# Mixer: backward turns beside the state sums, inputs a state ahead, one Silu block per pair, convolutions in the tail

## The reference, cut to what matters

```python
EMB, DS, DC, EXP = 128, 16, 4, 2          # DI = 256 channels, 16 states
def _mamba(x, in_w, conv_w, conv_b, xproj_w, dt_w, dt_b, A_log, D, out_w):
    xc, z = jnp.split(jnp.einsum('ble,ie->bli', x, in_w), 2, axis=-1)
    xc = _silu(causal_conv(xc, conv_w) + conv_b)          # DC = 4 taps
    dt, Bm, Cm = jnp.split(xc @ xproj_w.T, [DTR, DTR + DS], axis=-1)
    dt = jax.nn.softplus(dt @ dt_w.T + dt_b)
    A = -jnp.exp(A_log)
    dA = jnp.exp(dt[..., None] * A)                       # one decay per state
    dBx = dt[..., None] * Bm[:, :, None, :] * xc[..., None]
    h = dA_t * h + dBx_t                                  # the scan over time
    y = sum over the 16 states of h * C  + xc * D
    return (y * _silu(z)) @ out_w.T
out_f = _mamba(out, ...f weights)
out_b = _mamba(out[:, ::-1], ...b weights)[:, ::-1]
```

## Time and profile before

| what | us |
|---|---|
| median of 3 runs (3865.65 to 3873.80) | 3869.11 |
| the profiled execution, its time | 3876.9 |
| its span | 3875.1 |
| first scan of the mixer starts at | 1649.25 |
| last pair of the mixer ends at | 3383.34 |

### The profile page before, as it was taken

How to read it: one execution, slowest core, us unless ns; L and a number is a source line. 1 busy time by engine, 2 the same in 40 slices (tenths; PEclk the granted TensorE clock), 3 DMA queues, 4 the chain that set the end, 5 groups by cost and what they waited for, 6 DMA issues and landing times. The chain is left out here.

```text
span 3875.1 us, 60191 instructions
## 1 busy us (share of the span) xinstructions
PE 2899.2 (75%) x18634; PEld 2085.9 (54%) x18635; DVE 2717.1 (70%) x4018; ACT 2280.7 (59%) x4020; POOL 2070.9 (53%) x1444
## 2 busy tenths in 40 slices
PE   3999999521999960578888878888888887769934
PEld 2555555321666640256556656666566665669933
DVE  3788887442444447288888898888889898967643
ACT  1566665420333320499888888898888888522232
POOL 1011111265222222389889898888889898612234
PEclk6999999655999985799999999999999999879955
DMA  3444444411111136012222222222222222120050
GB/s 94 88 87 87 87 91 83 118 55 43 39 39 39 39 94 125 26 62 71 75 72 73 72 75 67 71 70 68 75 72 72 70 75 66 54 83 24 15 152 14
DMA packets 219679, 269.61 MB, mean 70 GB/s; under 512 B 36684, under 2 KB 139110, under 8 KB 214554
## 3 DMA queue, kind: packets, MB, share of 16 engines
q1 hardware_dynamic: 199106, 247.08, 24.6%
q0 software_dynamic: 12256, 18.82, 1.4%
q10 hardware_dynamic: 8064, 0.55, 0.2%
HBM read 219.79 MB, written 54.22 MB: 71 GB/s over the span
## 5 line engine op out<-in xcount | busy, mean ns | idle before, releaser
L1736 POOL TENSOR_TENSOR resid_x<-s_ux,s_B_rows 128x1024 f32<-128x1024 f32 x256 | 604.8, 2363 | 154.5 <-PE s_y L2084 154.4
L2013 DVE TENSOR_TENSOR_SCAN resid_x<-s_back_decay,s_back_in 128x1024 f32<-128x1024 f32 x256 | 584.2, 2282 | 143.9 <-PE s_back_in L2071 143.8
L2005 DVE TENSOR_TENSOR_SCAN resid_x<-s_dA,resid_x 128x1024 f32<-128x1024 f32 x256 | 582.4, 2275 | 114.3 <-ACT s_dA L1828 106.2
L2084 PE MATMUL s_y<-identity,resid_x 128*128 128x128 f32 x4096 | 560.9, 282 | 5.9 <-POOL resid_x L1744 5.9
L2084 PEld LDWEIGHTS s_y<-identity,resid_x 128*128 128x128 f32 x4096 | 499.7, 146 | 84.1 <-issue 52.1
L1744 POOL TENSOR_TENSOR resid_x<-resid_x,s_C_rows 128x1024 f32<-128x1024 f32 x192 | 453.3, 2361 | 44.4 <-DVE resid_x L2005 44.2
L1828 ACT ACTIVATE s_dA<-s_dt,s_A 128x510 f32<-128x510 f32 x512 | 330.4, 677 | 132.4 <-DVE resid_x L2005 132.1
L2020 DVE TENSOR_TENSOR resid_x<-resid_x,s_C 128x1024 f32<-128x1024 f32 x320 | 383.5, 1198 | 23.9 <-PE s_C L2061 23.3
L467 DVE TENSOR_REDUCE a_row_max<-a_maxscores 128x2 f32<-128x512 f32 x512 | 335.9, 683 | 79.5 <-PE a_maxscores L545 79.2
L1849 ACT ACTIVATE resid_x<-s_uT,s_bT 128x256 f32<-128x256 f32 x864 | 370.3, 496 | 10.3 <-issue 9.3
L391 ACT ACTIVATE a_probs<-a_scores 128x1024 f32<-128x1024 f32 x256 | 262.5, 1025 | 139.8 <-PE a_scores L558 135.4
(11 more groups left out here) (332 smaller groups left out, 5668.8 us busy)
## 6 DMA issues: line engine op xcount, KB each, us to landing
s_B_rows<-forward_rows SPq DMA_DIRECT2D x256, 256.0 KB, 3.3
s_C_rows<-forward_rows SPq DMA_DIRECT2D x192, 256.0 KB, 3.3
a_Q<-split_qk SPq DMA_DIRECT2D x96, 192.0 KB
split_qk<-a_parts SPq DMA_DIRECT2D x32, 384.0 KB, 2.8
e_x<-slot_inputs SPq DMA_DIRECT2D x135, 65.0 KB
a_K<-split_qk SPq DMA_DIRECT2D x64, 128.0 KB
f_mod_rows<-mod_rows SPq DMA_DIRECT2D x16, 512.0 KB, 9.9
c_y<-choice_outputs SPq DMA_DIRECT2D x16, 512.0 KB, 6.4
```

The source lines that it names most:

```text
L1736: tt(R[s, 0], ux[par][:], brow[s % BRING][:].unsqueeze(1).broadcast_to([P, C2, W]), ALU.mult).then_inc(S["in_ready"], 1)
L2005: nc.vector.tensor_tensor_scan(r, a, r, 0.0, ALU.mult, ALU.add).then_inc(S["scanned"], 1)
L2013: nc.vector.tensor_tensor_scan(r[:, ::-1], a[:, ::-1], b[:, ::-1], 0.0, ALU.mult, ALU.add).then_inc(S["scanned"], 1)
L2084: last = mm(YP[:, t, c2 * P:(c2 + 1) * P], R[s, d][:, c2, t * P:(t + 1) * P], core.ident[:], is_transpose=True, start=(s + d == 0 and t % ...
```

## The change

1. TensorE: `turn_input` for state s+1 moves from the head of chunk 2s+2 to chunk 2s+1, directly behind `add_up` of state s-1 and ahead of the skip products and the preps of that chunk.
2. ScalarE and GpSimd: `back_input` for state s+2 (before: s+1) is made in chunk 2s+1 (ScalarE before: chunk 2s). GpSimd makes its two tiles with one `tensor_tensor` of 128x512 in place of two `tensor_scalar` of 128x256.
3. ScalarE: the two Silu blocks of a pair (chunk 0 and chunk 11, four table loads) become one in chunk 31, with both directions of pair i+1 and the gate of pair i (two table loads).
4. The backward direction's convolutions move from chunks 0, 1, 6, 7 of iteration i to chunks 26 to 29 of the iteration before, the forward ones from 27 to 30 to 21 to 24; the waits on `PR` follow.
5. The other preps move: `bc` from chunks 14 and 15 to 6, `z` from 8 and 9 to 8 and 11, the later `dt` from 12 and 13 to 10 and 14, `turn_back` from 17 and 18 to 15 and 16. `OWN` is (4, 6, 9, 15), was (4, 7, 10, 15). GpSimd's preps start a chunk later and end two earlier.
6. Ahead of the loop all four convolutions of pair 0 are done, then its Silu.

```diff
-OWN = (4, 7, 10, 15)
+OWN = (4, 6, 9, 15)
-PE_NEXT = {**{27 + h: [("conv", 0, 0, 2 * h + k) for k in range(2)] for h in range(2)}, **{29 + h: ...
+PE_NEXT = {c + h: [("conv", d, k, 2 * h + tap) for tap in range(2)] for c, d, k in ((21, 0, 0), (23, 0, 1), (26, 1, 0), (28, 1, 1)) for h in range(2)}
-ACT_NEXT = {29: [("conv", 0, 0)], 31: [("conv", 0, 1)]}
+ACT_NEXT = {23: [("conv", 0, 0)], 25: [("conv", 0, 1)], 28: [("conv", 1, 0)], 30: [("conv", 1, 1)]}
...
 # GpSimd, back_input
-                    for k in range(POOL_TILES[s]):
-                        last = nc.gpsimd.tensor_scalar(bt[s % 2][:, k, :], uT[par][:, k, :], bT[par][:, k, s:s + 1], None, ALU.mult)
+                    tt(bt[s % 2][:, 0:n, :], uT[par][:, 0:n, :], bT[par][:, 0:n, s:s + 1].broadcast_to([P, n, DI]), ALU.mult).then_inc(S["bt_pool"], 1)
...
 # ScalarE, emit
-                        if c % 2 == 0:
-                            if s + 1 < DS and live(i, 1):
-                                back_input(i - 1, (u + 1) % 2, s + 1)
                         if c % 2:
+                            if s + 2 < DS and live(i, 1):
+                                back_input(i - 1, (u + 1) % 2, s + 2)
...
+                        if c + 1 == CHUNKS:
+                            if live(i, -1):
+                                silu(i + 1, (u + 1) % 2)
+                            if live(i, 0):
+                                silu_gate(i, u)
+                                nc.scalar.preload_act_table_set(EXP_TABLE)
...
 # TensorE, prep: the waits of z and dt
-                        if k == 0:
-                            pe.wait_ge(S["conv_read"], DIRS * C2 * (i + 1))
+                        if k == 0:
+                            pe.wait_ge(S["bT_read"], i + 1)
                         else:
-                            pe.wait_ge(S["z_read"], 2 * i + 1)
+                            pe.wait_ge(S["dt_read"], DIRS * C2 * i + 3)
...
 # TensorE, emit
-                            if live(i, 1):
-                                turn_input(i - 1, s)
...
                                 add_up(j, p, 1)
+                            if s + 1 < DS and live(i, 1):
+                                turn_input(i - 1, s + 1)
+                            if s + 1 == DS and live(i, 0):
+                                turn_input(i, 0)
```

More of the change, by code:

```diff
@@ L1494 @@
 EXP_TABLE = "natural_log_exp_and_others"
[L1495 to L1503, removed]
@@ L1504 @@
-ACT_NEXT = {29: [("conv", 0, 0)], 31: [("conv", 0, 1)]}
[L1505 to L1508, removed]
+PE_AT = {2: [("dt", 0, 0, k) for k in range(2)], 4: [("dt", 0, 1, k) for k in range(2)], 6: [("bc", d, k) for d in range(2) for k in range(2)],
+         7: [("bT", 0)], 8: [("z", 0)], 10: [("dt", 1, 0, k) for k in range(2)], 11: [("z", 1)],
+         14: [("dt", 1, 1, k) for k in range(2)], 20: [("uT", 0)], 25: [("uT", 1)]}
@@ L1954, in _ @@
                 turned(0)
-                conv(0, 0, 0, 0)
-                conv(0, 0, 0, 1)
+                for d in range(DIRS):
+                    for c in range(C2):
+                        conv(0, 0, d, c)
+                silu(0, 0)
+                nc.scalar.preload_act_table_set(EXP_TABLE)
                 def emit(i, u):
@@ L2136, in prep @@
                     if kind == "uT":
[L2137 to L2142 removed]
+                        if k and live(i, -1):
+                            pe.wait_ge(S["conv_read"], DIRS * C2 * (i + 1) + 2)
+                        elif k:
+                            pe.wait_ge(S["uT_read"], C2 * i + 1)
+                        elif live(i, -1):
+                            pe.wait_ge(S["x_read"], i + 2)
+                        else:
                             pe.wait_ge(S["out_read"], i - 1)
[L2144 to L2145 removed]
                         pe.wait_ge(S["u_ready"], DIRS * C2 * i + (C2 + k + 1))
@@ L2188, in _ @@
                 turned(0)
-                for c in range(C2):
-                    for k in range(DC):
-                        prep(0, 0, ("conv", 0, c, k))
+                for d in range(DIRS):
+                    for c in range(C2):
+                        for k in range(DC):
+                            prep(0, 0, ("conv", d, c, k))
                 def emit(i, u):
@@ L2197, in emit @@
                         past = live(i, 1) if s else live(i, 2)
-                        if c % 2 == 0:
-                            if past and p in OWN:
-                                c_rows(j, par, p, 1)
-                            if live(i, 1):
-                                turn_input(i - 1, s)
+                        if c % 2 == 0 and past and p in OWN:
+                            c_rows(j, par, p, 1)
                         if c % 2:
@@ L2214, in emit @@
                                 prep(i, u, what)
-                        if c in (17, 18) and live(i, 2):
-                            turn_back(i, i - 2, c - 17)
-                        if c == 19 and live(i, 2):
+                        if c in (15, 16) and live(i, 2):
+                            turn_back(i, i - 2, c - 15)
+                        if c == 17 and live(i, 2):
                             project(i - 2)
-                        if c == 23 and live(i, -1):
-                            pe.wait_ge(S["uT_read"], C2 * i + 1)
+                        if c == 19 and live(i, -1):
+                            if live(i, 2):
+                                pe.wait_ge(S["out_read"], i - 1)
+                            else:
+                                pe.wait_ge(S["dt_read"], DIRS * C2 * (i + 1))
                             turned(i + 1)
```

103 lines of the change are left out of this document (50 added, 53 removed).

## The result

| | before | after |
|---|---|---|
| median, four runs each (lowest, highest) | 3868.66 (3865.65, 3873.80) | 3913.07 (3905.98, 3920.88) |
| profiled execution, its span | 3876.9, 3875.1 | 3905.98, 3904.1 |
| mixer's first instruction on ScalarE to its last product | 1808.2 | 1846.4 |

The changed kernel is slower: ratio 1.0114, 95% interval [1.0089, 1.0139]. The side was predicted, the size was not: +20 us forecast, +44 measured on the medians.

The account below looks back on a forecast made before the run. Four engines nearly full, so waits between them bound the kernel. Walk, VectorE work 94.3 plus waits 14.3 plus clock 1.5 gives 110.1 a pair; 14 pairs and the ends add about 20 us: 3889, range 3830 to 3930.

Parts of the forecast that it names:

- Rival C: ScalarE: removed table loads also save a drain, 5.3 us a pair gained, 2.7 more than forecast; 3851; chance 0.03.
- Rival B: Whole pair: walked waits hide each other, pair 101, or half way 104.5; 3760 or 3809 us; chance 0.23.
- A: TensorE's clock no longer falls in a way that costs: pair 108.6, 3866 us, no change; chance 0.15.
- D: TensorE in the tail: low clock meets it, 4 us a pair in place of 1.5, 3924 us; chance 0.08.
- 1.5 for the clock on top: TensorE's clock still falls after long waits: 1.5 us a pair in place of 2.3.
- states 10 to 15, tail: Taps and uT behind each turn make turns 12 to 15, decays and a C row late: 4.3 us a pair.
- Silu block, state 1: ScalarE's 5.6 us block before the decays of state 1, mostly covered by VectorE: 1.8 us remain.
- bc, state 4: bc in one piece at chunk 6 delays turn 4, then bT, z and a C row: 2.3 us a pair.
- decays of states 6 to 9: ScalarE has 67 us of work against VectorE's 60, so decays come 0.7 to 1.5 late: 3.9 us a pair.
- z, turn_back, C rows, states 6 and 9: TensorE's second z and turn_back wait for ScalarE's step size; C rows come 0.9 and 1.1 late: 2.0 us.
- waits like the 3.01 go: Backward input turned as soon as the backward scan ends, so VectorE's waits for turned inputs, one of 3.01 us, vanish.
- 11 + 12 - 5: Mixer total: +11 us over 14 pairs, +12 at the start, -5 at the last pairs.

Follow-up runs that it names:

- experiment 1: Kernel before with only the early turn: 1.0172 of the kernel before; with the backward inputs made two states ahead as well: 1.0166.
- experiment 3: Kernel after with its turns put back late, rest of the new order kept: 1.0021 of the kernel before, pair 109.3.
- experiment 2: Twenty zero matmuls filling each of a pair's two long TensorE waits: in the kernel after 1.0119, in the kernel before 0.9972, both against the kernel before.

## Why the prediction was right and wrong

**What held.** The side; the start (first scan +12 counted from ScalarE's first instruction, +12 forecast; it began at 1572.27, 2.9 earlier than before, so the scan stands at 1658.36 and not at 1661); turned waits at 52.5 (some 50), decay waits at 84.9 (over 80), C row waits up; TensorE's waits of 3.04 and up to 3.8 for L1882; GpSimd's product:

```profile
L1752 POOL TENSOR_TENSOR resid_x<-s_uT,s_bT 128x512 f32<-128x512 f32 x73 | 76.5, 1047 | 0.0
```

It takes 1.05, near the lower bound, for two tiles of 0.91 each. It is worth nothing that experiment 1 can tell, and experiment 3 shows none for the pair of table loads that went. Rival C is out: in the kernel after the table load at 2437.26 takes 1.28 and Silu starts at 2438.55, 0.01 behind it, and even the whole block is worth only 1.5 a pair. Rival B is out, since the full order never came near 104.5. A is out, since the low clock stayed and the pair of 108.6 didn't come. D doesn't fit either: the granted clock is 0.93 where it was 0.95, but the kernel of experiment 3 has the same 0.93 with a pair as long as before.

**The step that failed** is the sum for a pair: "Sum 4.3 + 1.8 + 2.3 + 3.9 + 2.0 = 14.3, and 94.3 + 14.3 = 108.6", with 1.5 for the clock on top. Place by place, means over 13 pairs:

| place | forecast | measured |
|---|---|---|
| states 10 to 15, tail | 4.3 | 3.9 |
| Silu block, state 1 | 1.8 | 1.3 |
| bc, state 4 | 2.3 | 2.9 |
| decays of states 6 to 9 | 3.9 | 3.0 |
| z, turn_back, C rows, states 6 and 9 | 2.0 | 3.3 |
| state 0, stall in four pairs | none | 0.6 |
| sum of waits | 14.3 | 15.1 |
| lost beside each wait | none | 1.5 |
| small gaps, mostly 0.03 each | none | 0.7 |

VectorE's own work is 94.1, and 94.1 + 15.1 + 1.5 + 0.7 = 111.4. The waits themselves came out 0.8 above the forecast, and what the low clock makes of them (state 6 above) is in that 0.8, while the forecast had added 1.5 for it. So that term was too large. What I left out is the line below the waits. A wait costs more than the idle time that the trace shows:

```profile
2014.10 2.27 DVE L2009 TENSOR_TENSOR_SCAN resid_x<-s_dA,resid_x 128x1024 f32<-128x1024 f32 x1
2018.49 1.22 DVE L2024 TENSOR_TENSOR resid_x<-resid_x,s_C 128x1024 f32<-128x1024 f32 x1 [2.12 <-PE s_C L2065]
2020.24 2.29 DVE L2017 TENSOR_TENSOR_SCAN resid_x<-s_back_decay,s_back_in 128x1024 f32<-128x1024 f32 x1 [0.54 <-PE s_back_in L2075]
```

From the scan to the weigh is 4.39, less 2.12 of waiting 2.27, where without a wait it is 2.18: the overlap of neighbours is lost, 0.09 each time. The Trainium skill (Perfetto Trace Analysis, Optimizing Scalar/DVE Operations) says that half of the fixed cost that the profile shows for an operation overlaps with the next one; the rows agree, and show that a wait between the two takes it away. Before, 9.8 waits a pair made that 0.8 us; after, 17.2 short ones make it 1.5. My walk spread a similar lateness over more places and charged none for being a place. So of the 2.1 us between the pairs 1.1 is waiting, 0.7 their number, 0.35 the small gaps.

**Where I read the rows before wrongly.** I put the 2.3 us between the pair of 107.05 and the mean on the clock. The zeros in the kernel before give the clock some 1.1 of it (experiment 2). Another 0.8, 1.9 to 3.0 us in four of the 13 pairs, is a stall at state 0 of the next pair, in both kernels: its scan comes late though nothing that it reads is. In the kernel after, first VectorE, then GpSimd's inputs for states 0 and 1, then TensorE:

```profile
2437.64 2.29 DVE L2009 TENSOR_TENSOR_SCAN resid_x<-s_dA,resid_x 128x1024 f32<-128x1024 f32 x1 [1.92 <-POOL resid_x L1735]
```

```profile
2429.67 2.37 POOL L1735 TENSOR_TENSOR resid_x<-s_ux,s_B_rows 128x1024 f32<-128x1024 f32 x1 [1.51 <-PE s_y L2088]
...
2434.34 2.37 POOL L1735 TENSOR_TENSOR resid_x<-s_ux,s_B_rows 128x1024 f32<-128x1024 f32 x1 [1.29 <-PE s_y L2088]
```

```profile
2437.73 0.39 PE L2065 MATMUL s_C<-s_bc_parts,s_w_sel 96*128 96x512 bf16 x1 [1.61 <-issue]
```

The input of state 0 was ready at 2432.04, its decays at 2435.20, and both engines start together at 2437.7. The loop's body holds two pairs and runs five times, with the first four iterations and the last ones written out; the stall stands at the four places where the loop goes back to its start, and at none between the written-out pairs. So it belongs to the loop's end. What the engines do there no run tested. The pairs behind such a stall show no wait for the Silu block, which is why a few pairs of 109 looked like my walk's 108.6: they were not the clean ones, but those whose wait the pair before had paid.

**The early turn.** I wrote that "waits like the 3.01 go" and looked no further than the turn itself. They went, and experiments 1 and 3 show that this part is the loss: 1.7% alone, 0.9% in the new order. The prediction's place for it, C rows "0.9 and 1.1 late", was the right place and too small.

**The ends and the scale.** The last pair with prep beside it took 106.5, 0.8 less than before, where I had 5 less. In all the mixer took 38.3 more, where 11 + 12 - 5 gives 18: 16 of the difference are in the pairs and 4 at the end. What lies outside the mixer was 9 shorter in this profile, which no instruction of the change touches. The rest of the miss on the medians is difference between runs: the profiled execution before was 8 above its median, the one after 7 below its own. So some 15 of the 44 us on the medians are in no row of the two profiles.

## What to carry to other kernels

An instruction moved forward on an in-order engine must be priced by what it then stands in front of: moving the turn ahead took the cover away from one chunk of prep and put two in front of the C rows. Move it only where what stands ahead of it is itself waiting for another engine, and try the places singly: all sixteen turns early cost 0.9%, one of them alone gained 0.9%. When a walk over a new order gives many short waits in place of a few long ones, add the lost overlap for each; and before a difference between pairs is put on the clock, compare pairs of one trace at either clock, and kernels with the same granted clock. Matmuls of zeros test it only if they are shorter than the wait that they fill.

## What was not expected of the hardware

- A wait on VectorE costs 0.09 us beside its idle time (1.54 us in 17.2 waits a pair).
- GpSimd multiplies two tiles with a broadcast scalar column each in one `tensor_tensor` of 128x512 in 1.05 us; two `tensor_scalar` of 128x256 took 1.83.
- Twenty fp32 matmuls of 128x128 took 4.63 us at the full clock; with 29 such groups, each longer than the wait that it was to fill, the kernel after had a higher granted clock (0.96 for 0.93) and was no faster, 1.0119 against 1.0114.
- Where the loop of two pairs goes back to its start, four times, VectorE and TensorE both stand still, in the kernel after for 1.9 and 1.6 us; VectorE for up to 4.5 in the kernels with matmuls of zeros.
